# Attention outputs of six batches: from TensorE transposes to a round trip through DRAM

## Chip, cores, metric

One core of one Trainium2 chip. The metric is the device time of one execution in microseconds (us), lower is better.

## What is computed

Cut to what matters here. The kernel takes x (8, 128, 256), a context of the same shape and 8 lengths.

```python
xn = layernorm(x)                            # over the last axis, 256
qh, kh, vh = xn, ctx, ctx as (8, 8, 16, 256) # 8 heads of 16 rows, 256 positions
s = SCALE * log(k_length)                    # one number a batch
attn = softmax(s * einsum('bhdq,bhdk->bhqk', qh, kh), axis=-1)
x = x + einsum('bhqk,bhdk->bhdq', attn, vh)  # back as (8, 128, 256)
x = x + moe(layernorm(x))                    # shared FFN + 8 experts, top 1, capacity 128
```

A row of x (one of 128) is one dimension of one head, its 256 columns are the positions. So an output of attention, and the softmax sum that divides it, belong to a row (head, dimension) and a column (query position). After the first sum each row is a token of the FFN.

## The kernel before

All five engines run hand-written programs and meet in semaphores. The stage of the change is attention, from about 7 to 95 us. It is laid out in **turns** t = 0 to 41, and each engine's program is a loop over t (`for t in range(TAIL)`). There are 8 batches of 8 heads, 64 heads in all, two a turn, so four turns make a batch.

- TensorE (PE) in turn t: it weighs values (`weigh_values`, L1001, 8 matmuls) of an earlier turn; then the scores of heads 2t and 2t + 1 (`scores`, L964), interleaved with the shifted scores (`shifted_scores`, L985) of the two heads 7 turns back. LAG is 7, TURNS 32 and END 39. From t = 32 there are no new scores. Then come the transposes that the tables place in this turn.
- VectorE (DVE) takes two row maxima a turn (`maximum`, L523), each of a bank of PSUM. There are three such banks: scores of head n wait for the maximum of head n - 3. A batch's maxima are transposed (`turn_maxima`, L973), copied (`maxima_rows`, L758) and moved by two DMAs of SP into the queries (`load_maxima`, L294), which the batch's shifted scores wait for, three turns on.
- ScalarE (ACT) takes two exponentials a turn (`exponentials`, L765). They too have three banks: the shifted scores of head n wait for the exponential of head n - 3.
- A batch's outputs end in the bank O: for each head 16 rows of weighed values and 16 rows of the sum, the same sum 16 times. ACT copies O to `osum` (`copy_output`, L771, in turn 4b + 13).
- Then, in before: PE transposes `osum` in four pieces into bank X (`turn_output`, L1013, turn 4b + 14). DVE takes the reciprocal of the 16 sum columns (L530) and multiplies (`scale_output`, L535). PE transposes twice back (`turn_back`, L1021, turn 4b + 15), and DVE adds to xs (`add_attention`, L544).
- Then the token path: statistics on DVE (`token_stats`, L548, L550), two small activations on ACT (`token_rstd`, L775, L777), the normalised tokens x2 on GpSimd (POOL; L395) or DVE (L554, batches 6 and 7), their transpose on PE (`turn_tokens`, L1028), and the split in a high and a low part (`high_tokens` on ACT, L781; `low_tokens` on DVE, L559). Batch 7 goes the same way behind the loop.
- Bank X is shared: `X_USERS` lists its users in order, and each waits until the one before has been read (`x_free`).
- SP's queue issues, batch by batch, the maxima, and then an expert's weights (`load_expert`, for experts 1 to 4) or, for batch 4, the zeros of the expert rows. Expert 0's weights come behind the loop over batches.
- POOL also splits the shared weights in six pieces (`split_shared`, L402, L404) in turns 14 to 29.

```python
OUT_COPY, OUT_TURN, OUT_SCALE = turns(LAG + 6, 3), turns(LAG + 7, 4), turns(LAG + 7, 5)
OUT_BACK, OUT_ADD, STATS = turns(LAG + 8, 6), turns(LAG + 8, 7), turns(LAG + 8, 7)
TRSTD, TNORM = turns(LAG + 9, 8), turns(LAG + 9, 9)
TTURN, THI, TLOW = turns(LAG + 10, 10), turns(LAG + 10, 11), turns(LAG + 10, 12)
```

## Time and profile before

| | |
|---|---|
| time, median of 3 runs | 165.21 us (164.95 to 165.82) |
| the profiled execution | 166.03 us |
| its span, first to last instruction | 164.2 us |
| mean granted TensorE clock | 0.98 |
| turn 14's first transpose of outputs | 37.29 us |
| transpose of the first tokens / of batch 6's | 45.26 us / 95.53 us |

The span holds all that the engines did. 1.8 us of the profiled execution lie outside it. The stage of the change is from 35 to 96 us of the span. What follows it (the shared FFN, the routing and the experts) starts from TensorE's end of it.

### The profile page before, as it was taken

Reading aid. Unit: us, or ns where it says so; the run is one execution under the profiler, and the core shown is the slowest. Engines: PE = TensorE matmul, PEld = TensorE weight load, DVE = VectorE, ACT = ScalarE, POOL = GpSimd, SP = SyncE. Lnnn points to the kernel's source line nnn. Section 1 sums busy time; section 2 is a strip of 40 time slices with the busy share of each in tenths; the row PEclk is TensorE's granted clock in tenths of the full one; section 3 lists DMA queues with packets and bytes.
Section 4 is the critical chain, followed back from the end, with each engine's and each line's share of the span. In section 5 each row is a group of like instructions: output and inputs, shape, how many; then the busy total and the mean of one; then the engine's idle time right before and its main releaser. Section 6 shows DMA issues by size and latency. Waiting matters only on the chain.

```text
span 164.2 us, 3914 instructions
## 1 busy us (share of the span) xinstructions
PE 148.4 (90%) x1480; PEld 105.8 (64%) x1480; DVE 102.2 (62%) x250; ACT 87.1 (53%) x201; POOL 66.5 (41%) x88
## 2 busy tenths in 40 slices
PE   7498998998899999999999998999899799999940
PEld 7354554654555555555455677997799799989830
DVE  1488865669868786868141445779765687766220
ACT  3432237576646747475858369444542856465300
POOL 7162805800831806060303000045797277528350
PEclk9869999999999999999999999999999999999996
DMA  4990070718062430000080000002339928952110
GB/s 141 308 351 27 4 262 5 217 52 265 4 202 68 143 120 2 0 6 0 2 263 7 2 4 0 2 32 68 120 100 295 311 76 259 337 197 88 68 58 32
DMA packets 15699, 18.46 MB, mean 112 GB/s; under 512 B 1852, under 2 KB 14949, under 8 KB 15680
## 3 DMA queue, kind: packets, MB, share of 16 engines
q1 hardware_dynamic: 14240, 14.98, 28.7%
q0 software_dynamic: 1152, 2.97, 5.2%
q8 instruction: 12, 0.20, 0.5%
q10 hardware_dynamic: 288, 0.26, 0.5%
q14 instruction: 7, 0.06, 0.1%
HBM read 14.12 MB, written 4.21 MB: 112 GB/s over the span
## 4 chain that ended last, share of the span: by engine, by line
PE 70%; DVE 8%; ACT 6%; DMA 5%; issue 4%; POOL 3%; SPq 1%; POOLq 0%; ACTq 0%; DVEq 0%
PE bank L964 15%; PE bank L1001 10%; PE bank L985 9%; PE bank L1192 5%; PE bank L1133 4%; PE bank L932 4%; PE bank L1168 4%; PE bank L1169 4%; PE bank L1051 3%; PE bank L1053 3%; DMA wraw<-in_w 2%; DMA leni<-in_lens 2%; PE bank L1013 2%; PE bank L1028 2%; POOL qz L367 2%
## 5 line engine op out<-in xcount | busy, mean ns | idle before, releaser
L523 DVE TENSOR_REDUCE nm<-bank 128x2 f32<-128x512 f32 x64 | 40.9, 685 | 12.5 <-PE bank L964 12.5
L765 ACT ACTIVATE pt<-bank 128x512 f32<-128x512 f32 x64 | 34.5, 590 | 15.3 <-PE bank L985 15.1
L985 PE MATMUL bank<-qz,kz 32*128 32x256 f32 x256 | 41.3, 403 | 0.8 <-ACT pt L765 0.8
L964 PE MATMUL bank<-kz,qz 32*128 32x256 f32 x256 | 35.8, 421 | 2.4 <-POOL qz L367 2.4
L964 PEld LDWEIGHTS bank<-kz,qz 32*128 32x128 f32 x256 | 21.6, 192 | 13.2 <-issue 8.6
L985 PEld LDWEIGHTS bank<-qz,kz 32*128 32x128 f32 x256 | 24.9, 184 | 6.0 <-ACT pt L765 4.3
L1001 PE MATMUL bank<-pt,vext 128*32 128x256 f32 x256 | 20.2, 391 | 0.0
L367 POOL TENSOR_SCALAR qz<-xs,rs,mrs 128x256 f32<-128x256 f32 x14 | 7.7, 565 | 24.5 <-DVE mrs L490 24.5
L431 POOL DMA_INDIRECT expert_rows<-rk,idx_s x8 | 8.0, 1002 | 22.9 <-DVE rk L611 21.0
L392 POOL TENSOR_TENSOR mrs<-mv,rstd 128x1 f32<-128x1 f32 x6 | 1.1, 190 | 28.3 <-ACT rstd L777 28.3
L465 POOL DMA_INDIRECT out<-vext,rk x8 | 8.3, 1032 | 10.0 <-DMA vext<-out,rk 4.6
L1192 PE MATMUL bank<-wraw,kz 128*128 128x256 f32 (+1 forms) x48 | 11.8, 384 | 0.6 <-DVE rlo L659 0.3
L458 POOL DMA_INDIRECT vext<-out,rk x8 | 9.5, 1193 | 6.3 <-DMA out<-xs 4.1
L1192 PEld LDWEIGHTS bank<-wraw,kz 128*128 128x128 f32 (+1 forms) x48 | 8.7, 189 | 2.1 <-issue 0.6
L559 DVE TENSOR_TENSOR xlo<-bank,xhi 128x256 fp32r<-128x256 f32 x8 | 3.4, 424 | 10.7 <-ACT xhi L781 10.7
L1001 PEld LDWEIGHTS bank<-pt,vext 128*32 128x32 f32 x256 | 5.2, 108 | 6.7 <-issue 6.0
L744 ACT COPY vext<-bank 128x256 f32<-128x256 f32 x8 | 3.0, 372 | 11.8 <-PE bank L941 11.8
L1133 PE MATMUL bank<-shi,hThi 128*128 128x256 f32 x24 | 7.5, 314 | 0.9 <-DVE hTlo L639 0.9
L395 POOL TENSOR_SCALAR rk<-xs,rstd,mrs 128x256 f32<-128x256 f32 x6 | 7.3, 1223 | 0.6
L775 ACT ACTIVATE lnv<-mv,epst 128x1 f32<-128x1 f32 x8 | 2.4, 294 | 8.7 <-DVE mv L550 8.7
L1133 PE MATMUL bank<-slo,hThi 128*128 128x256 f32 x24 | 6.8, 283 | 0.0
L1133 PE MATMUL bank<-shi,hTlo 128*128 128x256 f32 x24 | 6.8, 282 | 0.0
(148 smaller groups left out, 322.3 us busy)
## 6 DMA issues: line engine op xcount, KB each, us to landing
wraw<-in_w SPq DMA_DIRECT2D x16, 352.0 KB, 3.9
wraw<-in_w SPq DMA_DIRECT2D x8, 256.0 KB, 3.9
expert_rows<-zero SPq DMA_DIRECT2D x1, 1032.0 KB, 5.6
out<-xs SPq DMA_DIRECT2D x8, 128.0 KB, 3.6
xs<-in_x SPq DMA_DIRECT2D x3, 256.0 KB, 6.0
cs<-in_ctx SPq DMA_DIRECT2D x3, 256.0 KB, 6.2
wraw<-in_w SPq DMA_DIRECT2D x8, 96.0 KB, 4.3
wraw<-in_sw SPq DMA_DIRECT2D x2, 352.0 KB, 5.0
```

Of the source, the lines that this page charges most:

```text
L367: nc.gpsimd.tensor_scalar(qz[:, b, half, :], xs[:, b, :], rs[:, b, half:half + 1], mrs[:, b, half:half + 1], ALU.mult, ALU.add).then_inc(q ...
L395: nc.gpsimd.tensor_scalar(x2[:, b, 0:D], xs[:, b, :], rstd2[:, b:b + 1], mrs2[:, b:b + 1], ALU.mult, ALU.subtract).then_inc(x2_made, 1)
L431: nc.gpsimd.indirect_dma_start(xd_dram, bass.IndirectOffsetOnAxis(ap=idx_s[:, b:b + 1], axis=0), x2[:, b, :], None, bounds_check=E * C - 1 ...
L458: nc.gpsimd.indirect_dma_start(res[:, e, :], None, out_rows, number(e), bounds_check=B * P - 1, oob_is_err=False).then_inc(gathered[e], 16)
L465: nc.gpsimd.indirect_dma_start(out_rows, number(e), res[:, e, :], None, bounds_check=B * P - 1, oob_is_err=False).then_inc(out_sent, 16)
L523: nc.vector.tensor_reduce(nm[:, b % 2, :, place], scores_bank[:].rearrange("p (u c) -> p u c", u=2), AX_X, ALU.max, negate=True).then_inc( ...
L765: nc.scalar.activation(pt[:, g % NPT, n % 4, :], sc_bank[n % NS][:], ACT.Exp).then_inc(exped, 1)
L964: mm = nc.tensor.matmul(scores_bank[:, u * D:(u + 1) * D], qz[rows, b, half, u * P:(u + 1) * P], kz[rows, b, half, :], start=True, stop=True)
L985: mm = nc.tensor.matmul(sc_bank[n % NS][:, c * D:(c + 1) * D], kz[rows, b, half, c * P:(c + 1) * P], qz[rows, b, half, :], start=True, sto ...
L1001: mm = nc.tensor.matmul(O[32 * j:32 * j + 32, g * D:(g + 1) * D], vext[:, b, c, h, :], pt[:, m % NPT, i, c * D:(c + 1) * D], start=(c == 0 ...
L1133: mm = nc.tensor.matmul(y_bank[b % 2][:, 0:D], hpart[:, b % 2, c * P:(c + 1) * P], weights(part, S2, D, c, D), start=(k == 0), stop=(k == ...
L1192: mm = nc.tensor.matmul(y_bank[(e + 1) % 2][:, 0:D], hTe[0:rows, e % 2, c * P:(c + 1) * P], wts[e % NW][0:rows, W2 + c * D:W2 + (c + 1) * ...
```

## The change

For batches 0 to 5 (MOVED = 6) the six transposes are left out. SP stores `osum`, 256 KB, to a DRAM tensor `sums`. Once that has landed (`o_sent`), it issues four loads of 64 KB that bring values and sums in natural rows into `onat` (`move_output`). DVE takes the reciprocal of the sums, which now are 128 x 256 numbers and not 128 x 16 (`invert_sums`). POOL multiplies and adds to xs (`scale_and_add`). Statistics, tokens and the rest follow later: for batch b < 5 the reciprocal is in turn 4b + 17, the tokens' transpose in 4b + 21; for batch 5 they are in turns 36 and 40. Batches 6 and 7 keep the transposes. POOL's form of the normalisation is multiply and add in place of multiply and subtract.

```diff
-OUT_COPY, OUT_TURN, OUT_SCALE = turns(LAG + 6, 3), turns(LAG + 7, 4), turns(LAG + 7, 5)
...
+OUT_COPY = [4 * b + LAG + 6 for b in range(B - 1)]
+MOVED = B - 2
+OUT_INVERT = [4 * b + LAG + 10 for b in range(MOVED - 1)] + [END - 3]
+STATS = [t + 1 for t in OUT_INVERT] + [END]
+TRSTD = [t + 2 for t in OUT_INVERT] + [END + 1]
+TNORM = [t + 2 for t in OUT_INVERT] + [END + 2]
+TTURN = [t + 4 for t in OUT_INVERT] + [END + 2]
+THI, TLOW = TTURN, [t + 5 for t in OUT_INVERT[:-1]] + [END + 1, END + 2]
+OUT_TURN, OUT_BACK = END - 1, END
...
+            def move_output(b):
+                n = b % 2
+                sp.wait_ge(o_copied, b + 1)
+                sp.dma_start(sums_dram[b], osum[:, n, :]).then_inc(o_sent[n], 16)
+                sp.wait_ge(o_sent[n], 16 * ring_pass(b, 2))
+                if b >= 2:
+                    sp.wait_ge(values_added, b - 1)
+                parts = sums_dram[b].rearrange("(j s d) (g c) -> s g j d c", j=4, s=2, g=2)
+                for half in range(2):
+                    for g in range(2):
+                        sp.dma_start(onat[64 * g:64 * g + 64, n, half, :], parts[half, g]).then_inc(o_moved[n], 16)
...
                 load_maxima(b)
+                if b >= 2:
+                    move_output(b - 2)
                 if b + 1 < NW:
                     load_expert(b + 1)
...
+            def scale_and_add(b):
+                pool.wait_ge(sums_inverted, b + 1)
+                nc.gpsimd.tensor_tensor(onat[:, b % 2, 0, :], onat[:, b % 2, 0, :], onat[:, b % 2, 1, :],
+                                        ALU.mult).then_inc(values_scaled, 1)
+                pool.wait_ge(values_scaled, b + 1)
+                nc.gpsimd.tensor_tensor(xs[:, b, :], onat[:, b % 2, 0, :], xs[:, b, :],
+                                        ALU.add).then_inc(values_added, 1)
...
+            def invert_sums(b):
+                dve.wait_ge(o_moved[b % 2], 64 * ring_pass(b, 2))
+                nc.vector.reciprocal(onat[:, b % 2, 1, :], onat[:, b % 2, 1, :]).then_inc(sums_inverted, 1)
...
-                    act.wait_ge(o_turned, b - 1)
+                    act.wait_ge(o_sent[b % 2], 16 * (b // 2))
```

How the rows of the engines move: first VectorE in the middle of the stage, one batch. Before (L523 is a maximum, two of them a turn; L530 and L535 scale, L544 adds, L548 and L550 are the statistics):

```order
L523 TENSOR_REDUCE nm<-bank 128x2 x4
L559 TENSOR_TENSOR xlo<-bank,xhi 128x256
L523 TENSOR_REDUCE nm<-bank 128x2 x2
L530 RECIPROCAL rinv<-bank 128x16
L535 TENSOR_TENSOR att<-bank,rinv 128x256
L523 TENSOR_REDUCE nm<-bank 128x2 x2
L544 TENSOR_TENSOR xs<-bank,xs 128x256
L548 BN_STATS st<-xs 128x6
```

The same of the changed kernel (L555 is the maximum, L574 the new reciprocal, L597 the low part of the tokens, L586 and L588 the statistics):

```order
L555 TENSOR_REDUCE nm<-bank 128x2 x6
L574 RECIPROCAL onat<-onat 128x256
L555 TENSOR_REDUCE nm<-bank 128x2 x2
L597 TENSOR_TENSOR xlo<-bank,xhi 128x256
L586 BN_STATS st<-xs 128x6
L588 BN_AGGR mv<-st 128x2
L555 TENSOR_REDUCE nm<-bank 128x2 x6
```

Two instructions of 16 and 256 columns in one turn, and the add in the next, became one reciprocal of 256 columns. It stands between the maxima of two turns, and the statistics follow one turn behind it.

Second, VectorE at the end of the stage, where no maxima are left. Before (from batch 5's last add to batch 6's statistics):

```order
L544 TENSOR_TENSOR xs<-bank,xs 128x256
L548 BN_STATS st<-xs 128x6
L550 BN_AGGR mv<-st 128x2
L559 TENSOR_TENSOR xlo<-bank,xhi 128x256
L530 RECIPROCAL rinv<-bank 128x16
L535 TENSOR_TENSOR att<-bank,rinv 128x256
L544 TENSOR_TENSOR xs<-bank,xs 128x256
L548 BN_STATS st<-xs 128x6
L550 BN_AGGR mv<-st 128x2
```

And now, from batch 4's reciprocal to batch 6's add (L562 and L565 are batch 6's scaling):

```order
L574 RECIPROCAL onat<-onat 128x256
L597 TENSOR_TENSOR xlo<-bank,xhi 128x256
L586 BN_STATS st<-xs 128x6
L588 BN_AGGR mv<-st 128x2
L574 RECIPROCAL onat<-onat 128x256
L586 BN_STATS st<-xs 128x6
L588 BN_AGGR mv<-st 128x2
L597 TENSOR_TENSOR xlo<-bank,xhi 128x256
L562 RECIPROCAL rinv<-bank 128x16
L565 TENSOR_TENSOR att<-bank,rinv 128x256
L579 TENSOR_TENSOR xs<-bank,xs 128x256
```

Batch 5's reciprocal and statistics (the second L574 and what follows it) now stand ahead of batch 4's low part (the second L597) and of batch 6's scaling.

Third, SP's queue from batch 3's maxima on. Before:

```order
L294 DMA qz<-mrow 4x256 [waits nm_row]
L294 DMA qz<-mrow 4x256
L307 DMA wraw<-in_w 128x2x352
L309 DMA wraw<-in_w 128x2x352
L313 DMA wraw<-in_w 128x2x256
L315 DMA wraw<-in_w 96x256
```

And now (L300 are the maxima, L307 the store, L314 the loads):

```order
L300 DMA qz<-mrow 4x256 [waits nm_row]
L300 DMA qz<-mrow 4x256
L307 DMA sums<-osum 128x512 [waits o_copied]
L314 DMA onat<-sums 64x1x256 [waits o_sent1]
L314 DMA onat<-sums 64x1x256 x3
L326 DMA wraw<-in_w 128x2x352
L328 DMA wraw<-in_w 128x2x352
L332 DMA wraw<-in_w 128x2x256
L334 DMA wraw<-in_w 96x256
```

The store and its four loads stand, with the wait for the store between them, ahead of the expert's weights.

## Rows read from the trace of the kernel before

**Rows 1.** the page's first part, busy time of each engine over the span

```profile
PE 148.4 (90%) x1480; PEld 105.8 (64%) x1480; DVE 102.2 (62%) x250; ACT 87.1 (53%) x201; POOL 66.5 (41%) x88
```

**Rows 2.** the chain that ended last, pieces in order: start us, us, what

```profile
45.26 0.44 PE bank L1028 x2
...
67.27 0.37 PE bank L1021 x2
...
69.28 0.31 PE bank L973 x2
...
80.66 0.43 PE bank L1028 x2
...
85.30 0.57 PE bank L1001 x8
85.87 1.06 PE bank L985 x8
...
88.74 0.37 PE bank L1028 x2
...
92.14 0.44 PE bank L1021 x2
...
95.53 0.38 PE bank L1028 x2
```

**Rows 3.** timeline of TensorE, turn 14: start, us, engine, line, operation

```profile
37.29 0.66 PE L1013 MATMUL bank<-cst,osum 128*128 128x128 f32 x4
```

**Rows 4.** lines kept apart by shape: busy us, mean ns, idle before

```profile
L548 DVE BATCH_NORM_STATS2 st<-xs 128x6 f32<-128x256 f32 x8 | 3.4, 427 | 0.3
...
L535 DVE TENSOR_TENSOR att<-bank,rinv 128x256 f32<-128x256 f32 x8 | 3.4, 425 | 0.3
...
L559 DVE TENSOR_TENSOR xlo<-bank,xhi 128x256 fp32r<-128x256 f32 x8 | 3.4, 424 | 10.7 <-ACT xhi L781 10.7
...
L530 DVE RECIPROCAL rinv<-bank 128x16 f32<-128x16 f32 x8 | 2.0, 249 | 2.8 <-PE bank L1013 2.8
...
L550 DVE BATCH_NORM_AGGREGATE mv<-st 128x2 f32<-128x6 f32 x8 | 1.5, 182 | 0.3
...
L605 DVE RECIPROCAL lrec<-lden 128x24 f32<-128x24 f32 x2 | 0.6, 296 | 0.0
...
L605 DVE RECIPROCAL lrec<-lden 128x16 f32<-128x16 f32 x1 | 0.2, 247 | 0.0
```

**Rows 5.** timeline around the start of turn 29: three engines and a wait

```profile
69.50 1.27 DVE L523 TENSOR_REDUCE nm<-bank 128x2 f32<-128x512 f32 x2
...
69.53 0.64 PE L1001 MATMUL bank<-pt,vext 128*32 128x256 f32 x8
...
70.05 1.07 ACT L765 ACTIVATE pt<-bank 128x512 f32<-128x512 f32 x2
...
70.69 0.18 PEld L985 LDWEIGHTS bank<-qz,kz 32*128 32x128 f32 x1 [0.16 <-ACT pt L765]
...
72.16 0.64 PE L1001 MATMUL bank<-pt,vext 128*32 128x256 f32 x8
```

**Rows 6.** lines by shape, GpSimd's two-input operations

```profile
L439 POOL TENSOR_TENSOR ew<-wraw,ew 128x704 fp32r<-128x704 f32 x4 | 6.7, 1700 | 0.0
...
L404 POOL TENSOR_TENSOR slo<-wraw,shi 128x365 fp32r<-128x365 f32 x4 | 3.9, 975 | 0.3
```

**Rows 7.** timeline of the DMA queue, the two writes of a batch's maxima

```profile
71.38 1.04 SPq L294 DMA_DIRECT2D qz<-mrow  x2
```

**Rows 8.** DMA issues: count, KB each, median us from issue to landing

```profile
out<-xs SPq DMA_DIRECT2D x8, 128.0 KB, 3.6
...
rk<-expert_rows SPq DMA_DIRECT2D x2, 129.0 KB, 2.1
rk<-expert_rows SPq DMA_DIRECT2D x1, 258.0 KB, 2.8
```

**Rows 9.** timeline of ScalarE, the copy of batch 5's sums

```profile
80.10 0.57 ACT L771 COPY osum<-bank 128x512 f32<-128x512 f32 x1
```

More of the change, by code:

```diff
@@ L107 @@
 MROW = [4 * b + 4 for b in range(B)]
[L110 to L111 removed]
+X_USERS = sorted([(t, "maxima", b) for b, t in enumerate(MROW)] + [(t, "tokens", b) for b, t in enumerate(TTURN)]
+                 + [(OUT_TURN, "output", MOVED), (OUT_BACK, "back", MOVED), (END + 4, "output", B - 1),
+                    (END + 5, "back", B - 1), (END + 6, "tokens", B - 1)])
 ROUTE = ("lmax", "ldif", "cand", "first", "oh", "cum", "pos", "past", "slot", "idx", "rec", "lsum", "ltwo",
@@ L922, in x_free @@
                     _, last, k = X_USERS[n - 1]
-                    pe.wait_ge({"maxima": nm_row, "output": scaled, "back": added, "tokens": x_lo}[last], k + 1)
+                    pe.wait_ge({"maxima": nm_row, "output": scaled, "back": added, "tokens": x_lo}[last],
+                               k - MOVED + 1 if last in ("output", "back") else k + 1)
             def unread(t):
```

58 lines of the change are left out of this document (36 added, 22 removed).

## The prediction

> **What bounds the kernel now.** I read the page first. TensorE is busy 90% of the span, VectorE 62% [rows 1]; but a share over 164 us says nothing of a stage, so the chain of waits came next. Between the first tokens' transpose (turn 17, 45.26 us) and batch 4's (turn 33, 80.66) every long piece is TensorE's. That is four batches in 35.4 us, 8.85 each [rows 2]. A turn without extras is 0.57 + 1.06 = 1.63 us [rows 2], so four are 6.5. The transposes add 0.66 and 0.37 (outputs), 0.31 (maxima) and 0.44 (tokens), with small overlaps [rows 2, 3]. Some 0.5 us a batch is left over.
>
> The timeline shows where that is. Turn 29 starts at 69.53, but the next turn only at 72.16 [rows 5]. Its shifted scores wait for an exponential (0.16 us at L985), because ScalarE started its exponentials only at 70.05. It had waited for the statistics, which VectorE ended just before its maxima at 69.50. So three engines move **in step**. With three banks each for maxima and exponentials, TensorE's third pair of scores in a turn needs the first maximum and the first exponential of the turn before. An engine that is more than about half a turn late stops TensorE, whatever its average load. That decides this change.
>
> **What goes.** 0.66 + 0.37, about 1.0 us of TensorE a batch, 5.8 us for six once the overlaps are taken off [rows 2, 3]. On VectorE go 0.25 + 0.42 and the add, which has the scaling's width, 0.42: 1.1 us a batch [rows 4].
>
> **What comes, and its price.** No row has a reciprocal of 256 columns. Those of 16 and 24 columns take 247 and 296 ns, 6.1 ns a further column; 296 + 232 x 6.1 = **1.71 us** [rows 4]. Below, it can't beat the 0.42 of another operation of 256 columns. Above, by the mean of the 24-column row, 12.3 ns a column, it would be 3.2. I take 1.71, since two rows of the same operation give the slope and the fixed part drops out, and 1.4 to 2.1 for the range. The Trainium skill (VectorE: DVE Perf Modes, the fixed hardware budget) says that a reciprocal divides iteratively, with a repeat count of 8. At eight cycles a column and the skill's 0.96 GHz that would be 2.2 us and some 2.6 us more in all than my sum; the trace's slope is nearer six cycles, and the sum goes by the trace.
>
> GpSimd's two operations: 975 ns at 365 columns and 1700 at 704, so 2.1 ns a column and 0.74 at 256 [rows 6]; two, with the semaphores, 1.6 us. GpSimd has room for them. Only VectorE's statistics wait for them. The new form of GpSimd's normalisation can only be quicker; nobody waits there now that the tokens come two turns later.
>
> The transfers: an issue on SP takes 0.5 us [rows 7]. 128 KB landed in 3.6 (a store, behind others) or 2.1, 258 KB in 2.8 [rows 8]. So 2.8 to 3.6 for the store, then four issues, the last 1.5 later, 2.1 to land: 6.4 to 7.2 us from the store's issue. In the middle of the stage the reciprocal comes four turns, 9 us or more, behind the copy, so this is hidden. SP's queue then issues up to 11 DMAs a batch, 5.5 us, and waits some 3 us for the store: within a batch's 9 us. The maxima stand in front of the store, so they are late only if the weights, now issued behind the loads, hold up those of the next batch (a rival below). ScalarE's next copy into the same half of `osum` waits for the store of two batches before, which is long over.
>
> **The middle: turns 17 to 33.** Time 0 is the end of turn 17's scores.
> 1. VectorE: two maxima 1.29 (1.27 and a gap [rows 5]), the reciprocal 1.71: 3.0.
> 2. Turn 18's maxima 1.29, batch b - 1's low part 0.42, the statistics 0.43 + 0.18 and gaps [rows 4]: 5.4. GpSimd's 1.6 us from 3.0 end at 4.6, beside the maxima.
> 3. ScalarE now takes its two small activations in turn 19, ahead of the exponentials, and waits for these statistics. In the old turn 29 it was 1.19 from the statistics' end (69.50) to the third shifted scores (70.69), and 1.05 more to the turn's end [rows 5]. So turn 20's scores end at 5.4 + 1.2 + 1.05 = 7.65.
> 4. Maxima transposed 0.31, turn 21 1.63: **9.6 us** for four turns. Before 8.85. TensorE's own work is about 7.3, so the transposes' gain is all eaten, and 0.74 a batch more. Four batches: **+2.9 us**. Each 0.1 us of the reciprocal moves this by 0.4.
>
> **The start: turns 14 to 17.** From 37.29 (turn 14's scores done, [rows 3]) to 45.26 [rows 2] are 7.97 us. The transposes of batch 0 go and its tokens come later. What stays is the statistics of the last queries: VectorE 1.29 + 2 x 0.43 with the small ones, about 2.1; ScalarE 1.2 as above; 1.05, 0.31, 1.63: 6.3. **-1.7 us**.
>
> **Turns 33 to 37.** No maxima are left, so VectorE is free. From 80.66 to 88.74 are 8.08 us [rows 2]. Now 0.42 + 4 x 1.63 = 6.94: **-1.1 us**.
>
> **The end: turns 38 to 41.** Time 0 is the end of turn 33's scores, where batch 5's copy ends too (80.10 + 0.57, [rows 9]). SP first issues the last maxima, so the store starts at 0.5 and the loads have landed at 6.9 to 7.7, say 7.3. VectorE waits for that with everything else behind it. Reciprocal to 9.0, GpSimd to 10.6, statistics to 11.25, and only then batch 4's low part, to 11.7. It frees bank X, and TensorE's transpose of batch 6's outputs needs X. TensorE could have had it at 6.94 + 0.42 + 1.63 = 9.0. It goes on at 11.75, transposes (0.6), has it scaled (0.8) and transposes back at 13.15. From turn 37's scores that is 6.2 us, where it was 3.4 (88.74 to 92.14): **+2.8 us**. Then the tokens of batch 5 (turn 40) and of batch 6 (41) follow each other through one bank, with a copy, a low part and a normalisation on VectorE between them: about 4.65 from the transpose back to batch 6's tokens, before 3.39 (92.14 to 95.53): **+1.3 us**.
>
> **The sum**: 2.9 - 1.7 - 1.1 + 2.8 + 1.3 = **+4.2 us**. What follows starts from TensorE's end of the stage, so I pass it on whole. The profiled execution took 166.03 us, which gives 170.2; the median before, 165.21, is 0.8 below it, and gives **169.4**.
>
> **Rivals.**
> - *TensorE's saving shows (faster).* For: TensorE is 90% busy, and 5.8 us of its work goes. It needs VectorE to hide the reciprocal. At 0.42 us the middle's period is 8.3 rather than 9.6, so -2.2 in place of +2.9, and the end loses 1.3 less: -2.2 in all, 163 us. It decides from a reciprocal of under 0.9 us, where my sum reaches zero (five reciprocals, each 0.8 shorter). Against: the slope in rows 4. Or the three banks carry more than I think, and the middle runs at TensorE's 7.3 + 0.5: -4.2 there and +1.3 for the rest as forecast, so **162.3 us**.
> - *Middle and end smaller (no change).* If the statistics don't stop ScalarE in turn 19, the middle's period is 9.1, +1.0. With a reciprocal of 1.4 it is -0.2, the start and turns 33 to 37 give -2.8, and the end costs 2.1 + 1.3 with loads that land at 6.9: +0.4, **165.6 us**.
> - *Transfers late in the middle (slower still).* Experts 3 and 4 and the zeros now go out just ahead of the next maxima, where they had been out for 5 us. If the maxima's writes queue behind 1 MB, about 4 us, three batches of shifted scores wait 1 to 1.5 us: **173 us**. For: the issue moves back by the whole round trip. Against: there are nearly three turns until they are used.
> - *The change doesn't do what it says*: if the loads are late every time and not only the last, VectorE waits in each batch. It needs over 9 us from copy to reciprocal; priced like the rival before.
>
> **Chances.** The forecast, 167 to 171.5: 0.66. Faster 0.15. About no change 0.09. Transfers late, or a reciprocal over 2.1: 0.10. The range of 80% runs from 164.3 (it leaves out the faster rival) to 172.6. About 0.5% is what a measurement of this kernel can tell from no change, so 164.4 to 166.0 is "the same": faster 0.15, same 0.07, slower 0.78.
>
> **What would show it.** Right: a reciprocal of about 1.7 us; GpSimd's two of 0.74; batches of 9.5 us in the middle with TensorE waiting for maxima in turns 19 and 20 and for exponentials in turn 20; in the last turns VectorE waiting for a DMA of `onat`, and TensorE over 2 us at the transpose of batch 6's outputs. Wrong: batches under 8.8 us, a reciprocal under 1 us, no wait before batch 6's outputs, or waits for the maxima's DMAs.

## The result, and the profile after

The changed kernel takes **177.59 us** (median of 4 runs, 174.84 to 182.18); the kernel before took 165.08 beside it (4 runs, 164.81 to 165.82). The ratio is 1.0586, interval [1.0526, 1.0645]. It rests on the two runs at 174.84 and 175.11; the other two, 180.06 and 182.18, ran at a lower clock of TensorE and are left out of it. The forecast was 169.4, range 164.3 to 172.6: the sign was right, the size was not. The profiled execution took 175.11 us, its span 173.2, against 166.03 and 164.2 before: 9.0 us of span to explain where the sum had 4.2.

The page of the changed kernel: busy time [rows 1], TensorE's granted clock in 40 slices of 4.3 us, three lines of groups (busy us, mean ns, idle ahead) and the store's landing:

```profile
PE 152.5 (88%) x1444; PEld 106.6 (62%) x1444; DVE 105.3 (61%) x238; ACT 88.3 (51%) x201; POOL 71.0 (41%) x100
...
PEclk9999999999969999999975599999999999999997
...
L422 POOL TENSOR_TENSOR onat<-onat 128x256 f32<-128x256 f32 x6 | 4.4, 725 | 27.3 <-DVE onat L574 27.3
L574 DVE RECIPROCAL onat<-onat 128x256 f32<-128x256 f32 x6 | 10.5, 1746 | 7.2 <-DMA onat<-sums 7.2
...
sums<-osum SPq DMA_DIRECT2D x6, 256.0 KB, 3.5
```

The two prices are as forecast: 1.75 us for the reciprocal (1.71), 0.73 for GpSimd's operation (0.74). But TensorE is busy for 4 us more, though it has 36 matmuls less, and the clock row has a 6 and further on a 7, 5, 5 that the kernel before doesn't have there. TensorE's transposes of tokens (L1076), of batch 6's outputs (L1061) and of these back (L1069) mark the stage, as in [rows 2] (start us, us):

```profile
53.69 0.44 PE L1076 MATMUL bank<-cst,rk 128*128 128x128 f32 x2
...
81.99 0.44 PE L1076 MATMUL bank<-cst,rk 128*128 128x128 f32 x2
...
91.39 0.69 PE L1076 MATMUL bank<-cst,rk 128*128 128x128 f32 x2
...
95.03 1.11 PE L1061 MATMUL bank<-cst,osum 128*128 128x128 f32 x4
...
97.09 0.69 PE L1069 MATMUL bank<-cst,att 128*128 128x128 f32 x2
...
102.91 0.44 PE L1076 MATMUL bank<-cst,rk 128*128 128x128 f32 x2 [0.96 <-DVE rk L592]
```

| piece, between ends of scores | before | after | difference | forecast |
|---|---|---|---|---|
| up to turn 14 | 37.29 | 36.73 | -0.6 | 0 |
| turns 14 to 17 | 7.97 | 6.23 | -1.7 | -1.7 |
| 17 to 33 (17 to 21: 10.73; then 9.43 each) | 35.40 | 39.03 | +3.6 | +2.9 |
| 33 to 37 (81.99 to 91.39) | 8.08 | 9.40 | +1.3 | -1.1 |
| 37 to batch 6's transpose back | 3.40 | 5.70 | +2.3 | +2.8 |
| from there to batch 6's tokens | 3.39 | 5.82 | +2.4 | +1.3 |
| from there to the end of the span | 68.7 | 70.3 | +1.6 | 0 |

What ended the waits (engine, line, what was waited for: us in all, times, longest):

```profile
DVE onat L574 <- DMA onat<-sums: 7.2, 2, 3.8
...
PEld bank L1033 <- DMA qz<-mrow: 3.9, 3, 1.7
...
ACT xhi L879 <- DMA wraw<-in_w: 3.1, 1, 3.1
...
PE bank L1033 <- DMA qz<-mrow: 2.7, 3, 1.3
```

VectorE waits for the loads twice, not once: for batch 5, as forecast, and for batch 4 as well. TensorE waits for the maxima's DMAs three times, which was a rival. What the list doesn't have is the forecast wait of TensorE ahead of batch 6's outputs: L1061 starts at 95.03 with no wait noted, straight behind turn 38's shifted scores. By then VectorE had done the low part that frees bank X for it:

```profile
94.27 0.39 DVE L597 TENSOR_TENSOR xlo<-bank,xhi 128x256 fp32r<-128x256 f32 x1
```

The chain of waits through turn 33 shows batch 4's whole way (start us, us, what; the pieces called issue, 0.02 to 0.07 us each, are left out):

```profile
72.81 3.55 DMA sums<-osum
76.38 0.54 SPq L314
...
78.09 4.33 DMA onat<-sums
82.45 1.76 DVE onat L574
84.29 0.74 POOL onat L422
85.09 0.73 POOL xs L425
85.85 0.44 DVE st L586
...
86.53 0.30 ACT lnv L822
86.96 0.59 ACT pt L812
```

From the store's issue to the last landing are 82.45 - 72.81 = 9.6 us, where the forecast had 6.4 to 7.2. The rest of that chain is the one that the forecast describes for the middle: reciprocal, GpSimd, statistics, and then ScalarE's exponentials behind its small activation. Table by stretch of 4 us (stretch, its length, busy us of PE, PEld, DVE, ACT, POOL, granted clock, DMA share, GB/s):

```profile
49.00:53.00 4.00, 4.00 (x42) 1.96 (x46) 1.86 (x3) 2.21 (x5) 2.27 (x5) 0.69 0.55 149
...
85.00:89.00 4.00, 3.47 (x32) 1.74 (x29) 0.61 (x2) 2.31 (x7) 1.56 (x4) 1.00 0.42 124
89.00:93.00 4.00, 4.00 (x26) 1.67 (x18) 1.75 (x1) 2.36 (x5) 0.77 (x2) 0.50 0.69 216
93.00:97.00 4.00, 4.00 (x24) 2.10 (x20) 1.60 (x5) 1.58 (x4) 1.50 (x3) 0.50 0.01 2
97.00:101.00 4.00, 4.00 (x27) 3.28 (x23) 1.03 (x3) 0.50 (x2) 0.00 (x0) 0.72 0.00 0
```

From 89.0 to 99.2 us the clock is 0.50, so TensorE runs at its lower level, 1.2 instead of 2.4 GHz. A turn there takes 3.02 us (92.01 to 95.03), where it took 1.63. Just before, TensorE stood still for only 0.5 us (87.06 to 87.59) and was busy for 3.47 of 4 us. There is a shorter such stretch from 48.0 to 51.4 us, behind a wait of 1.33 us for the maxima's DMA. No term and no rival of the forecast has the clock in it.

### The profile page after: what moved, and what is told of

It reads as the page before. It is cut to its first block, busy times and chain, and to the rows that moved or that the text cites. A ratio compares the mean times of both kernels' runs of the same rounds, so it can differ in the third digit from the quotient of the medians.

```text
span 173.2 us, 3864 instructions
## 1 busy us (share of the span) xinstructions
PE 152.5 (88%) x1444; PEld 106.6 (62%) x1444; DVE 105.3 (61%) x238; ACT 88.3 (51%) x201; POOL 71.0 (41%) x100
## 4 chain that ended last, share of the span: by engine, by line
PE 54%; DMA 15%; ACT 8%; DVE 7%; SPq 6%; issue 5%; POOL 2%; ACTq 0%; POOLq 0%; DVEq 0%
PE bank L1012 8%; PE bank L1033 8%; DMA qz<-mrow 7%; PE bank L1243 6%; PE bank L1219 5%; PE bank L1220 4%; PE bank L1049 4%; PE bank L1184 4%; PE bank L980 3%; DMA sums<-osum 3%; PE bank L1099 3%; PE bank L1101 3%; DMA onat<-sums 3%; SPq L300 2%; SPq L314 2%
## 5 line engine op out<-in xcount | busy, mean ns | idle before, releaser
L1033 PE MATMUL bank<-qz,kz 32*128 32x256 f32 x256 | 45.8, 430 | 4.5 <-DMA qz<-mrow 2.7
L555 DVE TENSOR_REDUCE nm<-bank 128x2 f32<-128x512 f32 x64 | 40.6, 680 | 13.9 <-PE bank L1012 13.7
L1012 PE MATMUL bank<-kz,qz 32*128 32x256 f32 x256 | 41.0, 415 | 2.4 <-POOL qz L388 2.1
L1033 PEld LDWEIGHTS bank<-qz,kz 32*128 32x128 f32 x256 | 27.2, 197 | 12.2 <-ACT pt L812 6.2
L1012 PEld LDWEIGHTS bank<-kz,qz 32*128 32x128 f32 x256 | 24.2, 188 | 14.9 <-issue 10.1
L1049 PE MATMUL bank<-pt,vext 128*32 128x256 f32 x256 | 21.9, 416 | 0.0
L422 POOL TENSOR_TENSOR onat<-onat 128x256 f32<-128x256 f32 x6 | 4.4, 725 | 27.3 <-DVE onat L574 27.3
L574 DVE RECIPROCAL onat<-onat 128x256 f32<-128x256 f32 x6 | 10.5, 1746 | 7.2 <-DMA onat<-sums 7.2
L490 POOL DMA_INDIRECT vext<-out,rk x8 | 9.0, 1123 | 8.2 <-DMA out<-xs 6.0
L706 DVE TENSOR_TENSOR rlo<-bank,rhi 128x256 fp32r<-128x256 f32 x8 | 3.4, 424 | 6.0 <-ACT rhi L892 5.9
```

The source lines that it names most:

```text
L490: nc.gpsimd.indirect_dma_start(res[:, e, :], None, out_rows, number(e), bounds_check=B * P - 1, oob_is_err=False).then_inc(gathered[e], 16)
L555: nc.vector.tensor_reduce(nm[:, b % 2, :, place], scores_bank[:].rearrange("p (u c) -> p u c", u=2), AX_X, ALU.max, negate=True).then_inc( ...
L574: nc.vector.reciprocal(onat[:, b % 2, 1, :], onat[:, b % 2, 1, :]).then_inc(sums_inverted, 1)
L1012: mm = nc.tensor.matmul(scores_bank[:, u * D:(u + 1) * D], qz[rows, b, half, u * P:(u + 1) * P], kz[rows, b, half, :], start=True, stop=True)
L1033: mm = nc.tensor.matmul(sc_bank[n % NS][:, c * D:(c + 1) * D], kz[rows, b, half, c * P:(c + 1) * P], qz[rows, b, half, :], start=True, sto ...
L1049: mm = nc.tensor.matmul(O[32 * j:32 * j + 32, g * D:(g + 1) * D], vext[:, b, c, h, :], pt[:, m % NPT, i, c * D:(c + 1) * D], start=(c == 0 ...
```

## The experiments

All ran with the kernel before beside them. Each time is a median; the range follows, since ranges turned out to matter. "Clock" is the granted clock over a whole run.

### The middle: is VectorE's lateness on the path?

**e2** leaves the round trip out: no store, no loads, ones in `onat`.

```diff
-                if b >= 2:
-                    move_output(b - 2)
...
+                if t == 11:
+                    nc.gpsimd.memset(onat[:], 1.0).then_inc(filled, 1)
```

> Leaves out the store and the four loads of each batch; the values and sums are ones that GpSimd writes once, so 1 is added in place of the attention output of batches 0 to 5. Reciprocal, multiply, add and all later steps stay. Theory A: the middle keeps its period of about 9.4 us between tokens' transposes, and only turns 33 to 41 gain, 5 us: about 170. Theory B: the middle falls below 9.0 as well, and with the end 7 to 9 us are gone: 166 to 168. Theory C (the granted clock, half of full speed from 88.7 to 98 us, follows from the stall at 86 us): without the stall the clock stays at full speed, which both A and B allow.

Profiled: 168.5 us, clock 0.992. The periods are 9.44 us throughout:

```profile
61.50 0.44 PE L1077 MATMUL bank<-cst,rk 128*128 128x128 f32 x2
...
70.94 0.44 PE L1077 MATMUL bank<-cst,rk 128*128 128x128 f32 x2
```

Turns 33 to 37 take 7.24, then 3.47 to batch 6's transpose back and 4.87 to its tokens. So without a single one of these transfers the middle's four periods are each 0.6 us longer than before: the step lock is there, and the transfers have no part in it. The other three runs of the same kernel took 177.8, 178.3 and 179.9 us at clocks of 0.917 to 0.928, so the clock can fall without any wait for the round trip.

**e1** cuts the reciprocal to 16 of its 256 columns and keeps all else.

```diff
-                nc.vector.reciprocal(onat[:, b % 2, 1, :], onat[:, b % 2, 1, :])
+                nc.vector.reciprocal(onat[:, b % 2, 1, 0:16], onat[:, b % 2, 1, 0:16])
```

> Leaves out 240 of the 256 columns of each reciprocal of the sums, so the values of those columns are multiplied by the sum and not divided. Everything else stays, the transfers too. Theory A (the engines in step: the reciprocal of 1.74 us on VectorE sets the middle's period of 9.43 us): the period falls by up to 1.5 us, to about 8.3, and the end gains 1.5: 6 to 7 us less in all, about 168.5. Theory B (the transfers set it: the maxima wait behind weights, and the loads of batches 4 and 5 land late): turns 19, 23 and 27 still wait for the maxima's DMAs, and the whole gains under 2.5 us, above 172.5.

173.84 us (170.17 to 177.81). The middle's periods are 11.16, 9.39, 12.94 and 8.37: no clean reading, because waits for the DMAs (9.8 us of `onat`, 6.3 and 5.1 of the maxima) and half a clock in the third took the reciprocal's place. **e6** has both edits, to take that away.

> The edits of e1_narrow and e2_no_transfers together: no transfers, ones in place of values and sums, 16 of 256 columns inverted. Theory A (the step of the engines): with a reciprocal of about 0.25 us the period falls from 9.44 to about 8.1 where nothing else holds the turn: 166.5 - 4 x 1.3 = about 161, and with fewer stops of TensorE the clock holds, so that the runs agree. If the period stays over 9: ScalarE's wait for the statistics, not the reciprocal, is what the step is made of.

164.98 us (163.8 to 167.25), ratio 0.9864 [0.978, 0.9947]. The first period is 7.96, the others 8.39. Against e2 that is 1.48 us in the first period and 1.05 in the others, for a reciprocal 1.5 us shorter: in the others 0.07 for each 0.1, where the forecast said that each 0.1 us of the reciprocal moves the middle by 0.4 over its four periods (that is 0.1 for 0.1). It also shows what this layout gives with the reciprocal and the transfers almost for nothing: 1.4% faster than before.

**e12** is the other way round: the kernel before with all its transposes, and the reciprocal added, on data that nobody reads (in turns 17, 21, 25, 29 and 33; the expectation counts them one too high).

```diff
+                if t in OUT_INVERT:
...
+                    nc.vector.reciprocal(unused[:], spare[:]).then_inc(unused_made, 1)
```

> The kernel before, all transposes kept, with one more reciprocal of 256 columns on data of its own in VectorE's queue in turns 18, 22, 26, 30 and 34 (where the changed kernel has it), which nobody waits for. Theory (engines in step, VectorE's time goes onto the path): 1.05 to 1.75 us more a batch, periods of 9.9 to 10.6 where 8.85 stood, 5 to 8 us more in all, 172 to 175 us. Rival (VectorE, busy 62%, takes it in its gaps): periods under 9.2 us and under 168 us.

169.1 us (167.7 to 171.14) against 164.77, ratio 1.0243 [1.0155, 1.0332]. The periods:

```profile
62.59 0.44 PE L1039 MATMUL bank<-cst,rk 128*128 128x128 f32 x2
...
65.60 0.63 PE L1024 MATMUL bank<-cst,osum 128*128 128x128 f32 x4 [0.93 <-DVE xlo L565]
...
72.40 0.44 PE L1039 MATMUL bank<-cst,rk 128*128 128x128 f32 x2
```

9.81 for 8.85 in three of the four periods (the first is 9.22): an instruction that nobody waits for costs 0.96 us a batch, although VectorE is idle for a third of the span. In turn 33, where no maxima are left, the fifth one costs nothing (8.03 us to turn 37). It is a little less than expected (9.9 to 10.6), and only the first period is near the rival's "under 9.2".

The wait by which it costs is not the one that the forecast has in the middle. The reciprocal makes VectorE's low part of the tokens late. That part frees bank X, and TensorE's transpose of outputs waits 0.93 us for it (the bracket). The changed kernel has no such transpose there. So e12 shows that lateness of VectorE reaches TensorE, here through bank X; that it does so through the banks of maxima and exponentials is shown by e2 and e6.

### The transfers

**e3** issues experts 3 and 4 and the zeros behind the loop; nothing else.

```diff
-                if b + 1 < NW:
+                if b + 1 < 3:
                     load_expert(b + 1)
...
             load_expert(0)
+            load_expert(3)
+            load_expert(4)
```

> The weights of experts 3 and 4 and the zeros of the expert rows are issued behind the loop over batches, so SP's queue holds only maxima and round trips in turns 12 to 32. Theory B: no shifted scores wait for a maxima's DMA any more; the first four turns from 42.96 fall from 10.7 to 9.5 us, but the later ones stay at 9.4, where statistics and exponentials are next in line: 1 to 2 us less, about 173.5. If the loads of batches 4 and 5 are late for the queue's sake too, 3 to 4 us more. Theory A: the same first gain, nothing else.

The waits for the maxima are gone, and the first three periods are 9.44 (the fourth, 10.05, ends at half a clock): the 1.3 us more in turns 17 to 21 came from the weights ahead of the maxima. VectorE's waits for `onat` stay (8.0 us, 2 times). The time is 177.13 us (173.43 to 178.88), ratio 1.0506 [1.0374, 1.0637], not clear of the changed kernel's 1.0586: in the profiled run TensorE had half its clock from 81.3 to 101.8 us. Its middle goes as that of e8, whose profiled run kept the full clock there.

**e5** reads 64 plain rows in each load, in place of four groups of 16 that lie 32 rows apart (same bytes).

```diff
-                parts = sums_dram[b].rearrange("(j s d) (g c) -> s g j d c", j=4, s=2, g=2)
...
+                        sp.dma_start(onat[64 * g:64 * g + 64, n, half, :],
+                                     sums_dram[b, 64 * g:64 * g + 64, D * half:D * half + D])
```

> The four loads of a batch read 64 plain rows of the DRAM tensor each, as many bytes in as many rows as before, but the wrong rows: reciprocals and products are of mixed values and sums. Theory F (the loads are slow for their shape: their source has 4 as its outermost count, and the trace shows the DMA engines 10 to 20% busy while they run): they land 1.5 to 3 us sooner, batch 4's stop at 86 us and the stop ahead of batch 6's outputs shrink by as much: about 171.5. Theory G (they are late because the store and SP's order are late): no change, 175.

174.28 us (171.14 to 177.8). TensorE's two waits for the maxima are 0.9 and 0.3 us (3.9 and 2.7 in the changed kernel), and turns 33 to 37 take 7.24 for 9.40. VectorE's waits for the loads of batches 4 and 5, in brackets:

```profile
78.21 1.75 DVE L574 RECIPROCAL onat<-onat 128x256 f32<-128x256 f32 x1 [0.95 <-DMA onat<-sums]
...
87.80 1.75 DVE L574 RECIPROCAL onat<-onat 128x256 f32<-128x256 f32 x1 [5.16 <-DMA onat<-sums]
```

Batch 4's way takes 7.2 us (its store was issued at 71.03) in place of 9.6, batch 5's 7.4 in place of 8.1. So the shape of the loads is most of what the forecast's 6.4 to 7.2 had left out. Batch 5 waits all the same: its wait is one of turns, as forecast. And here is the forecast wait of TensorE, at batch 6's outputs:

```profile
92.30 1.09 PE L1061 MATMUL bank<-cst,osum 128*128 128x128 f32 x4 [2.79 <-DVE xlo L597]
```

Within this wait the clock falls to 0.50, from 91.6 to 98.4 us. From turn 33's tokens to batch 6's e5 takes 20.83 us, the changed kernel 20.92: what batch 4's loads gain, batch 5's wait takes back.

In stretches of 1 us inside batch 4's loads the changed kernel moved 53 to 75 GB/s with the 16 engines busy for 0.15 to 0.21 of the time, e5 66 to 107 GB/s with 0.19 to 0.38. The Trainium skill (DMA: Bandwidth & Descriptors, Why a DMA increments its semaphore by 16 and not by 1) says that a DMA runs on the largest number of engines up to 16 that divides the slowest dimension (other than 1) of both sides. That would be 4 for the changed kernel's loads and 16 for e5's. By that rule, the trace agrees: the changed kernel's share stays under 0.25, four engines of 16, and e5's goes beyond it.

**e10** tries to get there with the rows that the kernel needs: eight loads of 16 rows.

```diff
+                parts = sums_dram[b].rearrange("(j s d) (g c) -> g j d s c", j=4, s=2, g=2)
+                for g in range(2):
+                    for j in range(4):
+                        first = 64 * g + 16 * j
+                        sp.dma_start(onat[first:first + 16, n, :, :], parts[g, j]).then_inc(o_moved[n], 16)
```

> The four loads of a batch become eight of 16 rows each, with both halves of the columns in one, so that the slowest dimension is 16 and not 4; same bytes, same 1 KB pieces. Theory (the load's shape keeps it to few DMA engines, and that is what holds up the maxima and the loads of batch 4): waits of TensorE for the maxima's DMAs under 1 us, periods of 9.4 us all through turns 17 to 33, turns 33 to 37 at about 7.3, the last load 2 to 3 us behind its issue; batch 5's wait of VectorE stays at 4 to 5 us, since eight issues take as long as they save; about 174 us. Rival (it is the four issues, the bytes or what else is queued, not the shape): waits of 3.9 and 2.7 us for the maxima as in the changed kernel, or longer with twice the issues, 177 us or more.

180.05 us (176.69 to 181.4), and the waits for the maxima are no smaller (4.8 and 3.6 us): the rival's outcome. The eight issues take 3.57 us where four took 2.21, batch 4's way still takes 8.1 us, and the weights go out later still. A load of 32 KB every 0.45 us is 73 GB/s, and 62 to 86 is what the trace shows: the issues have eaten what the shape gave. So this kernel can't tell how much the shape alone is worth; e5 can.

**e8** joins e3 and e5.

> e3_weights_late and e5_plain_loads together (the loads read the wrong rows). Theories B and F: no turn waits for maxima and the loads are in time, so this comes near e2_no_transfers's fast run, 168.5 to 170, with periods of 9.44. If the last batch's loads still land late, the round trip's fixed parts (store, wait, issues) are what is left: about 171.

175.69 us (172.88 to 179.94), ratio 1.0371 [1.0282, 1.046]. All periods 9.44, 7.24 for turns 33 to 37, and only batch 5's wait is left (4.8 us) — with half a clock behind it: 6.58 us from turn 37 to batch 6's transpose back and 6.39 to its tokens, where e2 has 3.47 and 4.87. Of those 4.6 us, 2.48 are TensorE's wait at batch 6's outputs (L1062, for the low part); the rest, 2.1, came at half a clock.

### The end

**e4** moves ScalarE's small activations and the normalisation one turn later, to take ScalarE's wait for the statistics away.

```diff
-TRSTD = [t + 2 for t in OUT_INVERT] + [END + 1]
+TRSTD = [t + 3 for t in OUT_INVERT[:-1]] + [OUT_INVERT[-1] + 2, END + 1]
```

> ScalarE's two small activations of batches 0 to 4, and GpSimd's normalisation, come one turn later, so that ScalarE doesn't wait for the statistics ahead of its exponentials. Theory A, as predicted: the period falls from 9.4 to about 9.0, 0.4 x 3, and batch 4's stop at 86 us goes too, with its clock: 1.5 to 4 us less. Theory B: nothing in the middle, since the maxima's DMAs hold the same turns; at most batch 4's stop.

178.41 us (176.88 to 182.37), ratio 1.0703 [1.062, 1.0786]. The periods are 8.98, 9.94, 9.61 and 8.62, 9.29 on average against 9.76: a little comes off, though the maxima's DMAs now stop TensorE for longer (5.5 and 4.2 us). Most of the lock stays when ScalarE's wait is moved away. The time of the whole kernel says nothing about the lock, because the edit makes a new stop. GpSimd's normalisation of batch 4 now stands behind batch 5's multiply, so TensorE waits for it through batch 5's whole round trip:

```profile
93.11 0.69 PE L1076 MATMUL bank<-cst,rk 128*128 128x128 f32 x2 [6.49 <-POOL rk L416]
```

**e9** puts batch 5 back on the six transposes, in its old turns. Batches 0 to 4 stay on the DRAM way.

```diff
-MOVED = B - 2
+MOVED = B - 3
...
-OUT_TURN, OUT_BACK = END - 1, END
+OUT_TURN, OUT_BACK = [END - 5, END - 1], [END - 4, END]
```

> Batch 5's outputs go back to the six transposes at the turns of the kernel before; batches 0 to 4 stay on the DRAM way. Theory (the end's stops come from batch 5 being too early for its round trip): the middle stays as it is in the changed kernel (late maxima included), turns 33 to 37 get the two transposes and take 9 to 9.9 us, then 3.4 us from turn 37's tokens to batch 6's transpose back and 3.4 to its tokens, where the changed kernel has 5.7 and 5.8; 4.5 us less, about 170.5 us, and if the clock stays full after turn 33 a turn there takes 1.63. Rival (the clock falls for other reasons than this wait): half clock between 80 and 100 us as in the changed kernel, 173 to 175 us.

From turn 33 to batch 6's tokens are 8.30 + 3.43 + 3.32 = 15.05 us, against 20.9 in the changed kernel and 14.9 before, at a full clock. That is 5.9 us, more than the 4.5 expected: the moved batch 5 costs the end its time, partly by its wait and partly by the clock behind it. The profiled run took 169.51 us, with half a clock from 46.5 to 53.3 us around a gap of 1.64 us in the middle; the others took 176.87, 179.14 and 184.48, at 0.89 to 0.94. The stage was mended, the median hardly moved.

### The clock

**e7** puts unread matmuls into twelve turns of the changed kernel, to keep TensorE dense.

```diff
+FILLS = {18: 3, 19: 3, 22: 3, 23: 3, 26: 3, 27: 3, 30: 3, 31: 3, 34: 2, 35: 4, 36: 4, 37: 4}
```

> The changed kernel with 2 to 4 matmuls of 512 columns, which nobody reads, at the end of the turns behind which TensorE waits (18, 19, 22, 23, 26, 27, 30, 31, and 34 to 37). Theory C (the granted clock falls to half because TensorE stands still in those waits, and costs 3 to 8 us): the clock of the core goes to over 0.98, the spread of the runs (174.8 to 182.2) closes to about 1%, and the time falls to 170 to 172, though the waits themselves stay and the added matmuls cost up to 1 us. Against it (the clock falls by the chip's state, whatever TensorE does): the clocks of the runs stay between 0.91 and 0.98 and the time doesn't fall.

177.87 us (175.32 to 179.26): the clock was higher (0.959 to 0.988), the time wasn't lower. Turns 33 to 37, with 14 of them, took 10.25 us at a full clock, for 9.40 in the changed kernel at partly half a clock: there TensorE had no time to give.

**e13** and **e14** change one thing in the kernel before: ahead of turn 37, TensorE waits for GpSimd to multiply scratch six times, or twice.

```diff
+                if t == END - 2:
...
+                        nc.gpsimd.tensor_tensor(spare[:], spare[:], spare[:], ALU.mult).then_inc(stopped, 1)
...
+                if t == END - 2:
+                    pe.wait_ge(stopped, 6)
```

> The kernel before, with one stop of TensorE put in by itself: ahead of turn 37 TensorE waits for GpSimd, which starts at the end of turn 36's scores and multiplies 256 columns of scratch six times (0.73 us each): some 4.5 us in which TensorE does nothing, as it does for batch 5's round trip in the changed kernel. Theory (a stop costs its own length and then the clock): the granted clock shows 0.50 for 5 to 10 us behind the stop, turns there take up to 3.0 us where they took 1.63, and the kernel is 6.5 to 10 us slower than before. Rival (a stop costs its length): clock 1.00 behind it, 4.5 us slower, less what of GpSimd's and VectorE's work it hides.

> As the last one with two multiplications: a stop of 1.6 us at the same place, the length of the stops of TensorE in the middle of the changed kernel. Theory (short stops don't cost the clock by themselves): clock 1.00 behind it, 1.6 us slower than before, within 0.5. Rival (each stop risks the clock, whatever its length): 0.50 behind it in the profile, or runs that lie 5 us and more apart.

177.95 us (176.53 to 178.73) and 174.12 us (173.9 to 175.81), against 167.49 (166.27 to 169.12, 17 runs). Both stops came out 1.3 to 1.4 us longer than meant, since GpSimd first ended a normalisation: 5.75 and 2.99 us. The timeline of TensorE in e14 (the stop in brackets), and its table by stretch:

```profile
89.00 1.08 PE L1012 MATMUL bank<-pt,vext 128*32 128x256 f32 x8 [2.99 <-POOL spare L426]
```

```profile
87.00:89.00 2.00, 0.00 (x1) 0.00 (x1) 0.00 (x0) 0.12 (x1) 1.87 (x3) 1.00 0.00 0
89.00:93.00 4.00, 4.00 (x22) 1.87 (x26) 0.00 (x0) 1.47 (x3) 0.00 (x0) 0.50 0.00 0
93.00:97.00 4.00, 4.00 (x24) 2.10 (x20) 0.62 (x2) 1.55 (x4) 0.00 (x0) 0.50 0.01 2
97.00:101.00 4.00, 4.00 (x30) 2.98 (x26) 2.28 (x8) 0.50 (x2) 0.00 (x0) 0.72 0.02 4
```

From turn 33's tokens to batch 7's the kernel before takes 20.78 us (80.64 to 101.42), e14 27.95, e13 30.79. Less the stops, **4.2 us** in both: TensorE works at half a clock for some 10 us behind either (89.0 to 99.2 in e14, 92.4 to 102.8 in e13). So e13's theory holds; e14's theory, that a short stop is free, was not tried at 1.6 us, and at 2.99 it is wrong.

What the shorter stops of the middle do (two turns out of four last 1.1 us longer than TensorE's own work; the gaps without any matmul are 0.35 to 0.5 us) is told by **e11**, **e15**, **e17** and **e18**. e11 is e9, e10 and e3 in one: its maxima are never late, and nothing stops it at the end. Its two runs at a full clock have a ratio of 1.0178 [1.0129, 1.0228] to before.

> Both of the last two changes, and experts 3, 4 and the zeros behind the loop: the version with all that the experiments so far point to. Theory (what is then left is the start's gain of 1.7 us against four periods that are 0.6 us longer): no DMA wait of onat or of the maxima, 8.0 to 8.6 us for turns 33 to 37, the rest as in the kernel before; 0.7 to 1.5 us over the kernel before at a full clock, 168 us on this chip. Rival (the clock): with stops of TensorE in each period the granted clock falls somewhere, and it takes 172 us or more.

e15 adds four unread matmuls behind turns 23, 27 and 31, where TensorE stops next.

```diff
+                if t in (23, 27, 31):
+                    pe.wait_ge(x_lo, (t - 19) // 4)
+                    for _ in range(4):
+                        nc.tensor.matmul(X[:].rearrange("p (n c) -> p n c", c=P), onesb[:],
+                                         onesb[:].unsqueeze(1).broadcast_to([P, 4, P]), start=True, stop=True)
```

> The best version so far (batches 5 to 7 on transposes, eight loads of 16 rows, experts 3, 4 and the zeros behind the loop), with four unread matmuls of 512 columns behind turns 23, 27 and 31, where TensorE stops for VectorE anyway. It ran at 167.4 and 167.7 us with the clock at 0.99, and at 180 and 182 with 0.91. Theory (the clock falls because TensorE has 1.1 us of stop in two turns out of four): with half of the stops filled the clock stays at 0.98 or more in most runs, and the time is 167.5 us, since the matmuls lie in the stop. Rival (other causes, or half the stops are enough to bring it down): half of the runs again at 178 us and more.

e17 and e18 are the same two kernels once more, on one chip.

> The kernel of e11 word for word, beside the filled one on the same chip. Theory (its stops of 1.1 us in two turns out of four let the clock fall in some executions): some of the 12 runs at 0.91 to 0.93 and 178 us or more, the others at 167.5. Rival (the chip of e11's call was at fault, and the fill of e15 did nothing): all runs within 3 us of 167.5.

> The kernel of e15 word for word, on the chip of e17. Theory: no run under a clock of 0.975 and none over 170.5 us, as in e15's 12, while e17 has such runs here. Rival: it spreads as e17 does.

| kernel | runs | median (range), us | runs under a clock of 0.93 |
|---|---|---|---|
| e11, unfilled | 4 | 173.87 (167.4 to 181.78) | 2 |
| e17, unfilled | 12 | 170.25 (166.69 to 180.65) | 5 |
| e15, filled | 12 | 167.84 (167.12 to 169.36) | 0 |
| e18, filled | 12 | 168.05 (166.42 to 172.54) | 0 |
| before, beside e17 and e18 | 22 | 166.59 (164.63 to 168.66) | 0 |

On one chip 5 of 12 runs lie at 177.5 us and more without the fill, and none with it; one filled run (172.54, clock 0.971) is over the 170.5 that I had set. Without the runs at a lower clock the ratios to before are 1.0073 [1.0001, 1.0144] (e17) and 1.0084 [1.0032, 1.0136] (e18). The matmuls cost nothing: at a full clock e17's and e18's best runs are 166.69 and 166.42. I have no profile of one of e17's long runs. Those that were profiled at such a clock, e3 (0.922) and e10 (0.918), show where it was in theirs, and it may be the same place in e17; the clock row of e10:

```profile
PEclk9999999999998799995555699999999999987997
```

It falls at the end of the middle, around turn 33, and stays down for some 20 us.

The other kernels agree, as counts. Where the middle keeps its period of 9.44 and nothing is filled in (e2, e3, e5, e8, e11, e17), 15 of 32 runs lie under a clock of 0.93. Where it is 8.4 (e6, e16), none of 10 does. The length of a gap alone doesn't decide it: e4 kept the full clock behind one of 1.84 us in the middle, e9 lost it around one of 1.64, and the four runs of e12, with a gap of 0.93 in three of its periods, are at 0.981 to 0.996. Why some executions fall and others don't is not shown.

### A version that beats both

In the DVE timeline of e11 the reciprocal is one block of 1.74 us behind turn 25's maxima, and TensorE's next two turns last 2.7 us (62.73 to 65.42, 65.42 to 68.20) for 1.63:

```profile
60.81 1.29 DVE L558 TENSOR_REDUCE nm<-bank 128x2 f32<-128x512 f32 x2 [1.06 <-PE bank L1017]
62.01 1.74 DVE L577 RECIPROCAL onat<-onat 128x256 f32<-128x256 f32 x1
63.67 1.22 DVE L558 TENSOR_REDUCE nm<-bank 128x2 f32<-128x512 f32 x2
```

If lateness within a turn is what counts, and not load, the same work in two pieces should cost less. **e16** is e11 with the reciprocal in halves of 128 columns in two turns that follow each other; GpSimd's operations are cut alike, and what follows comes a turn later.

```diff
+INVERT_REST = [t + 1 for t in OUT_INVERT[:-1]] + OUT_INVERT[-1:]
+STATS = [t + 1 for t in INVERT_REST] + [END - 4, END]
...
+                nc.vector.reciprocal(onat[:, b % 2, 1, 0:P], onat[:, b % 2, 1, 0:P]).then_inc(sums_inverted, 1)
...
+            def invert_rest(b):
+                nc.vector.reciprocal(onat[:, b % 2, 1, P:D], onat[:, b % 2, 1, P:D]).then_inc(sums_inverted, 1)
```

> The version of e11 (batches 5 to 7 on transposes, eight loads of 16 rows, experts 3, 4 and the zeros behind the loop, no fill), with the reciprocal of a batch cut into two halves of 128 columns in two turns that follow each other, GpSimd's operations cut alike, and the small part, the statistics, the two small activations and the normalisation one turn later. Theory (what stops TensorE is VectorE being over half a turn late in one turn, not its load): two reciprocals of 0.95 us in turns of 1.29 us of maxima leave each turn at 1.7 to 2.3 us, the period falls from 9.44 to 8.2 to 8.6 us, TensorE's stops shrink below 0.5 us and the clock stays up in all runs; with the start's 1.7 us that gives 3 to 4 us less than e11, 1.5 to 3.5 us under the kernel before. Rival (VectorE's sum of a batch is what counts, or the statistics stop ScalarE as before): periods of 9.2 us and more, the time of e11.

**164.68 us** (163.35 to 166.26, 6 runs, no clock under 0.983) against 166.59 beside it: ratio 0.9823 [0.9745, 0.9901], 1.8% faster than the kernel before (the interval leaves open whether it is 1% or 2.5%). Timelines of VectorE and of TensorE's tokens:

```profile
58.98 1.29 DVE L562 TENSOR_REDUCE nm<-bank 128x2 f32<-128x512 f32 x2 [0.67 <-PE bank L1025]
60.27 0.95 DVE L581 RECIPROCAL onat<-onat 128x128 f32<-128x128 f32 x1
61.40 1.29 DVE L562 TENSOR_REDUCE nm<-bank 128x2 f32<-128x512 f32 x2 [0.17 <-PE bank L1025]
62.60 0.94 DVE L585 RECIPROCAL onat<-onat 128x128 f32<-128x128 f32 x1
63.46 1.22 DVE L562 TENSOR_REDUCE nm<-bank 128x2 f32<-128x512 f32 x2
```

```profile
59.29 0.44 PE L1089 MATMUL bank<-cst,rk 128*128 128x128 f32 x2
...
67.72 0.44 PE L1089 MATMUL bank<-cst,rk 128*128 128x128 f32 x2
```

The period is 8.43 us (8.59 in the first; 8.2 to 8.6 expected), although VectorE does more in it: two reciprocals of 0.95 for one of 1.75. That is 1.0 less than e11's and 0.4 less than before. So VectorE's sum of a batch is not what counts. One thing is not separated: e16 also moves the low part, the statistics and the small activations a turn later. e4, which moved only the activations and the normalisation, came to 9.3 on average. The idea of the change pays, then, in this form: part of TensorE's saving shows once no engine is late by more than it can make up within a turn.

## Why the prediction was wrong in size

By its own steps, in the profiled run: start -0.6, middle +0.7, turn 33 to batch 6's tokens +3.1, what follows +1.6. These add up to the 4.8 us between +4.2 and +9.0. Two steps failed: the clock, a term put at nothing, and the landing of the loads, mis-sized.

- **The prices** of the reciprocal and of GpSimd's operations: right (1.75 and 0.73 us). By the repeat count that the Trainium skill gives (VectorE: DVE Perf Modes, the fixed hardware budget), read as eight cycles a column, the estimate was 2.2 us; it measured 1.75, so the measurement decides for the trace's slope.
- **The step lock in the middle**: right. 9.43 for 9.6, as a mechanism shown by e2 and e16, and by e6 with its size. Where the forecast was rough is the slope: in three of four periods 0.7 of a lateness reaches the period, not all of it. Its rival, that TensorE's saving shows with a short reciprocal, has its 8.3 (e6: 8.39), only not here.
- **Turns 14 to 17**: right (-1.7).
- **"It goes on at 11.75, transposes (0.6), has it scaled (0.8) and transposes back at 13.15"** is the step that failed most. It prices a stop of TensorE at its length and all work behind it at the full clock, and nothing in the prediction says why. Measured is a clock of 0.50 from 89.0 to 99.2 us. The forecast wait of over 2 us at batch 6's outputs didn't happen in the profiled run: VectorE's low part had freed bank X at 94.66 (94.27 + 0.39), and TensorE, at half its clock, came there only at 95.03. The 5.7 us for 6.2 are TensorE's own work at half speed, so that this term came out near is luck. The wait itself is real: 2.79 us in e5, 2.48 in e8. An estimate of what the clock cost: at a full clock TensorE would go on at 94.66, and with e2's 1.47 (89.62 to 91.09) and 4.87 reach batch 6's tokens at 101.0 and not 102.91, so 1.9 us. In turns 17 to 21 the clock has a small part too. The other two runs of the changed kernel, at 0.907 and 0.921, took 5 to 7 us more, and they make the median 177.59.
- **"Four issues, the last 1.5 later, 2.1 to land: 6.4 to 7.2 us from the store's issue"** failed too. The price of a landing was taken from loads of plain rows [rows 8], and these loads have another shape. They took 4.3 us behind the last issue; the way took 9.6 us for batch 4 and 8.1 for batch 5. For batch 5 they had landed 8.3 us behind turn 33's scores (90.31 - 81.99), where the forecast had 7.3: about 1 us of the end. For batch 4 the forecast had the way hidden, and VectorE waited 3.4 us. It would have waited a little even at 7.2 us (e5: 0.95). This makes turns 33 to 37 late, but it is not 2.4 us of the miss, as the table by pieces suggests. Of that row 1.1 us is turn 37 at half a clock (2.74 us for 1.63), and the rest goes into batch 5's wait (e5).
- **The rival of late transfers** was real and happened beside the forecast, not in its place: the weights behind the slow loads delayed the maxima of batches 3 to 5, +1.3 us in turns 17 to 21 (e3, e5), about 0.4 of it the half clock behind the wait (an estimate: the matmuls behind the wait took 1.48 us, and 1.07 in e10 at a full clock). Less the shorter periods (4 x 0.17), the middle misses by 0.7. Its chance of 0.10 was too low: "for" stood the whole round trip ahead of the weights, and that trip was itself under-priced.
- **"What follows is passed on whole"**: it grew by 1.6 us, and the stage's beginning shrank by 0.6. In the profile of after the wait is ScalarE's for the last weights (3.1 us, 1.6 before); e11, with a stage as short as before, has it too (3.0) and a tail of 70.0 us. But 0.9 of the 1.6 us is there earlier, when SP issues the reads of the expert rows (26.2 us behind batch 6's tokens, 25.3 before). The cause wasn't tried, and stays open.

## What to carry to other kernels

Where engines work in step through a few buffers, cost an added operation by how late it makes its engine in that turn, not by the engine's idle share: 1.75 us in one piece cost 0.96 us a batch on an engine that was 62% busy (e12), and with two halves of it in two turns part of the transposes' saving showed (e16). Take a DMA's landing from a row with the same shape of access, and list what is queued behind it. Ask of a wait that you take away what stands next in line: batch 4's loads in time gained nothing, because batch 5's wait took it back. And look at TensorE's granted clock behind each new stop: one stop of 3 us cost 7.2.
